# A hint for the closing branch of four long loops in a state-space and mixture-of-experts kernel

## The reference

```python
xn = layernorm(x)                              # x: 16 x 1024 x 256
# branch 1, a selective state-space scan, 32 states for each of 256 channels
dt = softplus(xn @ dt_w.T + dt_b); A = -exp(log_A)
b = xn @ B_w.T + B_b;  c = xn @ C_w.T + C_b
h[t] = exp(A * dt[t]) * h[t-1] + (dt[t] * xn[t]) * b[t]
y[t] = sum_n(h[t] * c[t]) + D_skip * xn[t]
# branch 2, a mixture of 8 experts, 2 for each token, with a capacity
disp = tokens placed in slots of their experts (slots over the capacity dropped)
out = relu(disp @ w1 + b1) @ w2 + b2           # per expert, hidden size 1024
moe = sum_k gate_k * out[expert_k, slot_k]
result = x + y + moe
```

## Time and profile before

| | |
|---|---|
| time, median of 3 runs | 3767.57 us (3766.1 to 3768.28) |
| profiled execution, its own time | 3767.04 us |
| its span, first to last instruction | 3765.4 us |
| busy share | DVE 96%, POOL 88%, PE 83%, ACT 69% |
| granted TensorE clock, mean | 0.970 of 2.4 GHz |
| idle of DVE for ACT's copy of c (L893) | 21.7 us in 16 waits |
| idle of DVE for POOL's `u` (L1076) | 37.0 us in 35 waits |

### The profile page before, as it was taken

The page is one execution under the profiler, slowest core; times in us unless marked ns, Lnnn a source line. Parts: engine busy times, 40 slices in busy tenths (PEclk is TensorE's granted clock), DMA queues, the critical chain, the costliest instruction groups (busy, mean ns, idle before and its releaser), DMA issues.

```text
span 3765.4 us, 61761 instructions
## 1 busy us (share of the span) xinstructions
PE 3107.5 (83%) x16292; PEld 2071.8 (55%) x16292; DVE 3617.8 (96%) x2155; ACT 2597.3 (69%) x4949; POOL 3295.5 (88%) x1350
## 2 busy tenths in 40 slices
PE   7766888888888888888888888888888888888887
PEld 3354555555555555555555555555555555555554
DVE  7787999999999999999999999999999999999998
ACT  3345776777777777767777777777777777777776
POOL 2017999999999999999999999999999999999997
PEclk9988999999999999999999999999999999999999
DMA  8984556655656556555666555565556655565556
GB/s 294 349 153 140 165 165 169 177 129 166 171 172 177 163 158 169 157 153 160 169 175 174 165 164 148 162 163 168 165 167 176 172 158 137 175 170 161 165 165 172
DMA packets 345460, 645.43 MB, mean 171 GB/s; under 512 B 49561, under 2 KB 221597, under 8 KB 344797
## 3 DMA queue, kind: packets, MB, share of 16 engines
q1 hardware_dynamic: 252238, 539.29, 44.5%
q0 software_dynamic: 67776, 85.24, 13.5%
q10 hardware_dynamic: 25104, 16.91, 2.0%
HBM read 516.08 MB, written 142.80 MB: 175 GB/s over the span
## 4 chain that ended last, share of the span: by engine, by line
issue 41%; POOL 32%; DVE 8%; DMA 6%; PE 2%; POOLq 1%; ACT 1%; SPq 1%; DVEq 0%; ACTq 0%
POOL u L1076 21%; DVE h L1285 6%; POOL out_rows L1033 4%; POOL xg L1021 4%; DMA dtx<-dtx_rows 3%; DVE hc L1273 2%; POOL dt_n L999 2%; DMA out_rows<-o_sb,sidx 2%; PE bank L658 1%; DMA dtx_rows<-dtx_n 1%; PE bank L649 0%; ACT bank L818 0%; POOL out_rows L1038 0%; POOL dtx_n L1006 0%; POOLq L268 0%
## 5 line engine op out<-in xcount | busy, mean ns | idle before, releaser
L1076 POOL TENSOR_TENSOR u<-dtx,b_sb 128x2048 f32<-128x2048 f32 x512 | 2436.3, 4758 | 38.6 <-DVE h L1285 22.1
L1285 DVE TENSOR_TENSOR_SCAN h<-bank,u 128x1024 f32<-128x1024 f32 x1024 | 2291.4, 2273 | 39.6 <-POOL u L1076 37.0
L818 ACT ACTIVATE bank<-dt,a_neg 128x1024 f32<-128x1024 f32 x1026 | 1135.8, 1109 | 439.3 <-DVE h L1285 400.8
L649 PE MATMUL bank<-xgt,w_sb 128*128 128x256 f32 x4096 | 1018.9, 392 | 240.4 <-ACT ht L861 209.6
L1273 DVE TENSOR_TENSOR hc<-h,bank 128x2048 f32<-128x2048 f32 x514 | 1161.6, 2260 | 22.5 <-ACT bank L893 21.7
L649 PEld LDWEIGHTS bank<-xgt,w_sb 128*128 128x128 f32 x4096 | 743.5, 191 | 587.6 <-issue 505.4
L658 PE MATMUL bank<-w_sb,ht 128*128 128x256 f32 x4096 | 983.1, 395 | 51.5 <-ACT o_sb L880 51.5
L658 PEld LDWEIGHTS bank<-w_sb,ht 128*128 128x128 f32 x4096 | 796.0, 199 | 257.2 <-issue 149.9
L861 ACT ACTIVATE ht<-bank,b_sb 128x256 f32<-128x256 f32 x1024 | 423.3, 463 | 298.7 <-PE bank L649 298.7
L607 PE MATMUL bank<-hc,rsum 128*32 128x512 f32 x4112 | 547.8, 605 | 2.4 <-DVE hc L1273 2.4
L1033 POOL DMA_INDIRECT out_rows<-o_sb,sidx x258 | 415.5, 1610 | 51.4 <-issue 37.0
(11 more groups left out here) (129 smaller groups left out, 1881.6 us busy)
## 6 DMA issues: line engine op xcount, KB each, us to landing
b_sb<-bc_rows SPq DMA_DIRECT2D x258, 512.0 KB, 4.3
c_sb<-bc_rows SPq DMA_DIRECT2D x258, 512.0 KB
dt<-dt_rows SPq DMA_DIRECT2D x132, 512.0 KB, 6.5
dtx<-dtx_rows SPq DMA_DIRECT2D x132, 512.0 KB, 6.9
w_sb<-w SPq DMA_DIRECT2D x18, 1024.0 KB, 5.3
dt_rows<-dt_n SPq DMA_DIRECT2D x137, 128.0 KB, 3.8
dtx_rows<-dtx_n SPq DMA_DIRECT2D x137, 128.0 KB
out_rows<-y_sb POOLq DMA_DIRECT2D x34, 512.0 KB
```

Source lines behind the costliest of these rows:

```text
L649: mm = pe.matmul(m_ps[:, c, :], w1_sb[:, kk, ch * P:(ch + 1) * P], xgt[:, kk, :], start=(kk == 0), stop=(kk == KD - 1))
L818: act.activation(a_ps[k % 2], dt[:, k % GPP, :], ACT.Exp, scale=a_neg[:, col:col + 1]).then_inc(a_ready, 1)
L1076: pool.tensor_tensor(u[:, gp:gp + 2, :], dtx[:, gp:gp + 2, :], b_sb[:, j, :].unsqueeze(1).to_broadcast([P, 2, S]), ALU.mult).then_inc(u_re ...
L1285: dve.tensor_tensor_scan(h[:, k, :], a_ps[k % 2], u[:, k % UB, :], 0.0, ALU.mult, ALU.add).then_inc(scan_done, 1)
```

## The change

The four loops of 16 steps are opened by a helper that asks for a hint: one instruction at the head of the body, executed in every pass, that names the branch which closes the loop and says that it will likely be taken. The last of the eight passes falls through. Bodies, waits and counts stay. DVE's loops and the loops of the prologue have no hint.

```diff
+        def long_loop(eng):
+
+            return nc.Fori(0, E, engines=bass.OrderedEngineSet([eng.engine]), hint_back_edge=True)
+
...
-            with sp.Fori(0, E) as e:
+            with long_loop(sp) as e:
...
-            with pe.Fori(0, E) as e:
+            with long_loop(pe) as e:
...
-            with act.Fori(0, E) as e:
+            with long_loop(act) as e:
...
-            with pool.Fori(0, E) as e:
+            with long_loop(pool) as e:
```

## The result

The changed kernel takes 3745.01 us (median of 4, 3743.84 to 3746.07) against 3766.84 us before (median of 4). The ratio is 0.9943, 95% interval 0.9927 to 0.9959: 21.8 us less, where 15 were forecast, and 2 us outside the range. Two later comparisons, on two chips, gave 0.9937 (0.9924 to 0.9951) and 0.9946 (0.9933 to 0.9959). Lines behind the helper stand 4 higher in this kernel (L653 is the L649 of before).

What follows compares the result with a forecast made beforehand. DVE was taken as pacemaker, so only its waits could be won back. Span 3765.4 less 15.2 us for the edges is 3750.2, 3752.4 on the median's scale, forecast as 3752.5 us, range 3747 to 3757.

Steps and rivals of the forecast that it cites:

- What bounds it, and where the back edge hits: DVE paces the kernel; instruction fetches at seven back edges stall PE and ACT and make DVE wait, 2.17 us an edge.
- The net of the edges is 583.74 - 7 x 81.22 = 15.2 us: DVE's seven three-step stretches behind back edges, 583.74 us, would fall to the middle level of 81.22 each, saving 15.2 us.
- eight middle stretches: DVE's three-step stretches from step 8, mid-pass, same work without a back edge: 649.77 us, 81.22 each.
- The lower end of the range: 3747 us: all DVE idle time at the edges, about 20.7 us, goes and none returns as waits for POOL.
- ACT's stall lies within PE's ... alone it costs DVE the 0.51 us: At the back edge ACT's 3.69 us stall is hidden by PE's; alone it costs DVE 0.51 us ahead of the scan.
- The first copy: ACT's copy of c for DVE after a back edge, 4.94 us late, of which DVE's cover hides 2.33 us.
- POOL, SP, hint and exit at nothing: Hints on POOL and SP, the hint instruction (at most 1.6 us) and the loop exit (up to 1.8 us) counted as 0.
- POOL's 1.1 us: POOL's multiplication of the new pass starts 1.10 us after its engine was free; DVE does not wait for it there.
- No effect: Rival: what the hint fetches or notes is gone by the branch, edges stay at 83.39 us, time 3767.6; chance 0.16.
- the displaced block: Rival: the hint's fetch at the head displaces the following block, PE stalls twice per pass, 3785 to 3812 us; chance 0.07.
- the late case: Rival: PE still resumes more than 2.3 us late, or only the other engines' hints work, 3754 to 3767 us; chance 0.07.

Runs made afterwards that it cites:

- before_again: The kernel before, unchanged and without hints, run once more for a second profile: 3773.19 us against 3771.66, ratio 1.0002.
- pe_only: The hint on PE's loop alone, ACT, POOL and SP without, against the kernel before: 3762.25 us against 3770.63, ratio 0.9972.
- shift: The kernel before with one plain semaphore instruction at the head of each of the four loops, no hint: 3770.71 us against 3770.63, ratio 0.9994.
- pe_act: The hint on the loops of PE and ACT, POOL and SP without, against the kernel before: 3755.25 us against 3771.66, ratio 0.9951.
- hint_last_step: All four loops hinted, at the head of the last of 16 steps, some 26 us ahead of the branch: 3757.91 us against 3771.66 before, ratio 0.9961.

## Why the prediction was right in kind and wrong in size

**What bounds it, and where the back edge hits: right.** DVE is busy 97%, the gain that repeats with the hints lies in the stretches behind the back edges, and in them in step 0. The branch fell to 0.45 us (0.1 was said), and the first fill is again on time at full clock. The granted clock over the whole first step 0 is 1.00 where it was 0.89, and from 755 to 762 us, about as far into the step as the earlier trace rows, 1.00 where it was 0.57.

```profile
755.00:762.00 7.00, 5.44 (x31) 3.85 (x32) 7.00 (x4) 5.83 (x14) 6.64 (x5) 1.00 0.64 170
```

**The failing step is "The net of the edges is 583.74 - 7 x 81.22 = 15.2 us".** Its mechanism held, the term was mis-sized. It took the eight middle stretches of one profile for the level to which the edges would fall, and that profile had the second longest middle of 14. With PE and ACT hinted at the head or at step 8, seven profiles have edges of 563.2 to 565.6 us, 564.2 on the mean, 80.60 each. The three without any hint have 585.2, 83.61 each. The term is then 585.2 - 564.2 = 21.0 us and not 15.2: 1.5 more from the higher start and 4.3 more from the lower level. Of these 4.3, 2.5 are that profile's long middle (81.22 against 80.86 on the mean of all 14). In the other 1.8 the hinted edges are shorter than even the mean middle; why is open. Against the three measured differences of 21.8, 22.3 and 18.8 us it leaves little that needs another cause. The 5.1 us of the middle and the 2.5 us of the prologue in the first pair of profiles need no hint: without any the middle is also 645.07 us, and the first scan of the changed kernel comes anywhere from 325.2 to 331.9 us, that of the kernels without a hint from 327.7 to 332.0. A small part of the middle may be POOL's hint (see before_again).

**The lower end of the range fell with it.** 3747 us was the sum of DVE's idle at the edges, 20.7 us, with none coming back. Idle time understates what a wait costs: two scans in a row take 4.46 us and one alone 2.28, so one that follows without a wait starts 0.1 us before its predecessor's recorded end, and a wait loses this too. In the seven steps 0 of before the excess was 207.23 - 183.75 = 23.5 us: 20.5 of them are idle, as was estimated, and 2.9 are recorded as busy. What came back at step 1 is 5.2 us. And the time also drifts by chip and execution by a few us, which a range made of one profile's terms had not in it.

**"ACT's stall lies within PE's ... alone it costs DVE the 0.51 us": wrong.** It was read from a trace in which PE's stall was there and hid it. With PE's gone, ACT's alone keeps the edges at 578.2 instead of 563.7 us, 2.1 us an edge. At the first edge of pe_only the way can be followed: ACT empties late, PE stands and slows down, and the decays and the second copy come late. How the 2.1 us divide between these isn't shown. It didn't hurt the sum, which had both stalls gone. The first copy, on which the argument was built, is indeed in time.

**POOL, SP, hint and exit at nothing: right.** shift costs nothing and pe_act has the full edges. POOL's 1.1 us stayed in the trace after, as a wait for a transfer. That POOL's hint brings nothing at all isn't shown (2 us in the middle stretches stay open). Behind the last pass nothing is late: from the last scan's end to the end of the span it is 21.3 us, and was 21.2, and the branch that falls through takes 88 ns.

**The rivals.** No effect is refuted by the branch of 0.45 us, and the displaced block by fewer instruction packets (144 and 198 before, 138 and 141 after), not more. Part of the late case can be made by hand: hint_last_step. The Trainium skill's sentence that prefetch is purely sequential (Runtime: NRT & Kernel Launch, Instruction fetch mechanics) does not hold for a hinted branch here: with it PE goes on 0.45 us behind the branch, without it 5.5 us.

## What to carry to other kernels

When a long unrolled loop closes, look for waits on "issue" that come as often as the back edge, on every engine, and price them by comparing stretches with and without the edge on the engine that paces the kernel. Take that comparison from more than one profile, or keep the spread of the stretches in the range. A stall that lies beside a longer one on a partner engine is not covered but only second in the queue: at the edges, hinting PE alone gave 7.0 us, ACT alone 0.2, both together 21.6; so mend both before judging either, and put the hint well ahead of the branch.

## What the runs showed of the hardware that was not expected

- A closing branch whose head has to be fetched held PE 4.6 to 6.0 us. The next instruction of ACT's sequencer came 2.9 to 4.1 us behind the branch, SP's 5.1 to 5.7 and POOL's 5.8 to 6.4. With the hint it is 0.5 us on PE and SP, 0.4 on ACT and 0.3 on POOL.
- The hint needs a lead, and not the same on each engine. 26 us ahead is enough for PE (0.46 us), and not for the others, which are as late as without a hint (hint_last_step); 210 us is enough for all four. The Trainium skill (Advanced Engine Details and Errata, ISA Cache) gives TensorE four times the instruction memory of the others; that fits the difference, but no run here varied it.
- The hints save fetches. These are queue 14's packets over the whole run with the hint on ACT alone, on PE, ACT and SP, on PE, ACT and POOL:

```profile
q14 instruction: 191, 1.56, 0.1%
```

```profile
q14 instruction: 184, 1.51, 0.1%
```

```profile
q14 instruction: 148, 1.21, 0.1%
```

From 198 without hints, ACT's hint saves 7, SP's another 8 on pe_act's 192, and POOL's 44 on the same, over six per back edge. With the hint at step 15 on all four the count is 191, as with ACT's alone. Why POOL's saves so much is not settled; the time that it may have brought is not told apart from none.
- Queue 8 falls from 144 to 138 with PE's hint and with no other, so it is PE's, as was taken.
- The slow group behind a wait of PE isn't sure to come. Of the seven first groups behind the back edges before, after waits of 1.94 to 3.35 us, five take 2.67 to 3.75 us and two 1.96 and 1.97. Behind the seven edges, step 0 takes 28.2 us twice, with the granted clock at 1.00, and 29.5 to 30.7 us five times, with 0.89 to 0.94; so the dear edges are those in which the clock fell. In pe_only, where ACT and no fetch makes PE wait (2.54 us at the first edge), the group behind is as slow as the earlier trace rows.
